# Cross-attention on one core: the output projection on split operands with source parts of their own, linear sums two blocks side by side, context loads issued by ScalarE, one place per tile

## The chip, the core and the metric

The kernel runs on one core of one Trainium2 chip. Its time is the device time of one execution in microseconds, and the number compared is the median of several executions. An engine has its own instruction queue and meets the others only at semaphores. The names here: PE or TensorE (matmuls), DVE (VectorE), ACT (ScalarE), POOL (GpSimd), SP (SyncE, which here only issues DMAs).

## The reference

Four batches of 1024 rows of width 512, and a context of the same size. First a 16-head softmax attention of x over the context, with an output projection, a residual and a layer norm; then a linear attention of the result over the same context, with a residual and a second layer norm.

```python
# first layer
Q, K, V = x @ Wq.T + bq, ctx @ Wk.T + bk, ctx @ Wv.T + bv      # 16 heads of 32
att = softmax(Q K^T / sqrt(32));  out = (att V) @ Wo.T + bo
x = layernorm(out + x) * gamma0 + beta0
# second layer
Q_phi, K_phi = elu(x), elu(ctx)
KV = einsum('bnd,bne->bde', K_phi, ctx)
Z = 1 / (Q_phi . K_phi.sum(axis=1) + 1e-6)
x = layernorm(x + (Q_phi @ KV) * Z) * gamma1 + beta1
```

All is float32. Where products must be both quick and accurate, the kernel splits an operand into a high part, rounded to the form fp32r, and a low part (the rest), and adds three products: high x high, high x low, low x high.

## The kernel before, in words

A **unit** is one batch, one group of four heads (128 columns) and one chunk of 256 rows of x: 4 x 4 x 4 = 64 units. A unit has 16 **ticks**, numbered k over the whole run (1024, named HALVES). In a tick TensorE does one product of scores for the row maxima (`pass1`, L464, 512 columns), and 26 ticks later (LEAD) one pair of transposed scores (`pass2`, L478, 2 x 256 columns); ACT takes the exponential of the latter into a ring `p_ring` (L640), DVE the maximum of the former (L775). Three score banks and two transposed-score banks lie between the engines. Every eight ticks TensorE makes a `visit`: the weighted values of four exponentials (L496) and their row sums (L503), for which POOL adds pairs of `p_ring` (L1036) and pairs of pairs (L1043; DVE does half, L813).

Everything else is put **beside** the score products, at most one piece in a tick, none in a visit's tick. A planner in plain Python, run when the kernel is built, writes this order. It knows chains with a number of pieces (LENGTH): K, V, Q projections (4, 4 and 2), O the output projection of a tile of 128 rows (4), T the transposes of its features (1), A its linear attention (4), S a block of 128 rows of the linear sums KV (8), N the total of the context features (1), B the bias through Wo (4). A chain writes one of two PSUM banks, `misc`, in turn. Of the chains that are ready it takes the one with the earliest deadline; `earliest` and `deadline` are given in ticks. `book` puts the steps of DVE, ACT and POOL into ticks where a budget has room, `send` does so for SP's DMAs; `bulk` transfers are kept out of ticks 2 to 7 of each unit and out of ticks 13 to 23. Every engine's program is a loop over k that emits what is booked there, so a wait in one instruction holds up all that follows it on its engine.

**Keys and queries** go through DRAM to be stacked as high, low and high rows: `put_keys` (L1202) after ACT's `k_high` and DVE's `k_low`, then `stack_keys` (L1210); `put_queries` (L1171) and `stack_queries` (L1179). The row maxima take the same road (L1187, L1192).

**Linear sums**: `context_features` on ACT makes relu and exp of a 128 x 128 block of `ctx_nat` into `f_sb` (L713, L716), on DVE the elu into `fphi_sb` (L952); `sum_kv` on TensorE is one fp32 product for each of 8 context tiles (L574), for 4 blocks of each batch; POOL adds the features into `phi_total` (L1090, L1094). `load_context` on SP (L1220) brings a batch's eight tiles once; ACT waits for all eight before the first feature.

**Output projection**: `normalise` on DVE transposes and inverts the row sums through `den_rows` and writes `outT`, a ring of 19 units (L835). `o_project` (L549) multiplies it in full fp32 by `wo`, `sum_y` (L874) adds x and the bias, which POOL has added to x (L1050). The first norm, the features `e_sb` (ACT, L682 and L687; DVE, L911), the `dot` with `phi_total` (L917, which writes its unused products over x_nat), T (L557), A (L566, three fp32r products each piece) and the second norm follow. A tile holds two places, `x_nat` and `y_sb`, in three slots, and in the last batch four more slots in `ctxT_sb`; the last four of the eight last tiles reuse slots:

```python
slot_of = [tile % NX for tile in range(TILES - KT)] + [NX, NX + 1, NX + 2, NX + 3, 0, 1, 2, NX]
```

## Time and profile before

| what | value |
|---|---|
| median of 3 runs | 1534.6 us (1530.89 to 1534.61) |
| profiled execution, its own time | 1535.64 us |
| its span | 1534.0 us |
| mean granted clock of TensorE | 0.996 |
| TensorE busy | 1495.3 us (97%) |
| VectorE, ScalarE, GpSimd busy | 1200.1, 825.5, 1130.6 us |
| data moved by DMA | 170.16 MB |

The span is the time from the first to the last instruction. A busy share says how long an engine had an instruction in it, also while that instruction was held up; which engine sets the pace of a stretch is seen in the stretch, and in the chain of work that ended last, which is followed back from the last instruction.

### The profile page before, as it was taken

What the parts mean: (1) busy time and instruction counts of PE and PEld (TensorE: products, weight loads), DVE (VectorE), ACT (ScalarE), POOL (GpSimd) and SP (SyncE); (2) the same over time, 40 slices, a digit from 0 to 9 for tenths busy, and PEclk for the clock granted to TensorE, in tenths of its full rate; (3) what the DMA queues carried; (4) which work ended last, traced back from release to release, by engine and by line L of the source; (5) the groups of instructions that cost most, each with busy time, mean ns of one, the idle gap of its engine ahead of it and who ended that gap; (6) DMA issues with size and microseconds to landing.
All of it is one profiled execution on the core that took longest, in us unless ns stands there. A gap on an engine that the chain in (4) does not pass through costs nothing.

```text
span 1534.0 us, 30583 instructions
## 1 busy us (share of the span) xinstructions
PE 1495.3 (97%) x11040; PEld 1053.0 (69%) x11040; DVE 1200.1 (78%) x2445; ACT 825.5 (54%) x1595; POOL 1130.6 (74%) x1036
## 2 busy tenths in 40 slices
PE   8899999999999999999999999999999999999986
PEld 6666767676766767667677777766767677756653
DVE  6577787767787887977787787888677778798987
ACT  2454565545555555665555555656555555565542
POOL 0366676757888787957678888876678887796995
PEclk9999999999999999999999999999999999999999
DMA  6735164352434245253343534325342342421001
GB/s 219 200 122 148 55 184 127 120 134 86 129 93 131 84 127 155 59 145 118 102 107 98 143 93 131 122 90 142 102 139 76 119 133 87 143 65 34 14 23 41
DMA packets 159573, 170.16 MB, mean 111 GB/s; under 512 B 20288, under 2 KB 122048, under 8 KB 159424
## 3 DMA queue, kind: packets, MB, share of 16 engines
q1 hardware_dynamic: 157696, 167.16, 36.8%
q8 instruction: 88, 1.44, 0.4%
q10 hardware_dynamic: 1728, 1.05, 0.2%
q14 instruction: 61, 0.50, 0.1%
HBM read 125.97 MB, written 42.21 MB: 110 GB/s over the span
## 4 chain that ended last, share of the span: by engine, by line
PE 85%; DVE 4%; POOL 4%; DMA 3%; issue 2%; ACT 1%; SPq 1%; DVEq 0%; POOLq 0%; ACTq 0%
PE score L464 15%; PE scoreT L478 14%; PE acc L496 14%; PE misc L537 7%; PE misc L513 7%; PE misc L526 6%; PE misc L574 6%; PE misc L549 6%; PE misc L566 5%; PE acc L503 3%; POOL pair_sum L1036 2%; DVE maxes L775 1%; PE misc L557 1%; DMA k_dram<-k_low 1%; DMA ctx_nat<-ctx_in 1%
## 5 line engine op out<-in xcount | busy, mean ns | idle before, releaser
L640 ACT ACTIVATE p_ring<-scoreT 128x512 f32<-128x512 f32 x1024 | 596.9, 595 | 572.1 <-PE scoreT L478 568.5
L1036 POOL TENSOR_TENSOR pair_sum<-p_ring 128x512 f32<-128x512 f32 x512 | 659.7, 1301 | 306.8 <-DVE pair_sum L813 165.0
L775 DVE TENSOR_REDUCE maxes<-score 128x1 f32<-128x512 f32 x1024 | 683.7, 680 | 196.5 <-PE score L464 190.7
L464 PE MATMUL score<-k_stack,q_stack 96*128 96x512 f32 x1024 | 601.0, 588 | 4.8 <-DVE maxes L775 1.8
L478 PEld LDWEIGHTS scoreT<-q_stack,k_stack 104*128 104x128 f32 x2048 | 387.2, 191 | 160.9 <-ACT p_ring L640 87.7
L478 PE MATMUL scoreT<-q_stack,k_stack 104*128 104x256 f32 x2048 | 419.2, 286 | 9.3 <-ACT p_ring L640 8.6
L464 PEld LDWEIGHTS score<-k_stack,q_stack 96*128 96x128 f32 x1024 | 193.1, 189 | 158.0 <-issue 109.8
L496 PE MATMUL acc<-p_ring,v_sb 128*32 128x256 f32 x4096 | 247.6, 382 | 0.0
L496 PEld LDWEIGHTS acc<-p_ring,v_sb 128*32 128x32 f32 x4096 | 120.0, 109 | 83.4 <-issue 0.4
L1043 POOL TENSOR_TENSOR pair_sum<-pair_sum 128x512 f32<-128x512 f32 x128 | 165.7, 1295 | 0.0
L537 PE MATMUL misc<-wv,ctxT_sb 128*128 128x128 f32 x1024 | 134.5, 274 | 0.0
L526 PE MATMUL misc<-ctxT_sb,wk 128*128 128x512 f32 x256 | 131.4, 596 | 1.9 <-DMA ctxT_sb<-ctxT_in 1.7
L574 PE MATMUL misc<-ctx_nat,fphi_sb 128*128 128x512 f32 x256 | 131.9, 596 | 0.2 <-DVE fphi_sb L952 0.2
L513 PE MATMUL misc<-xT_sb,wq 128*128 128x256 f32 x512 | 131.5, 379 | 0.2 <-DVE k_low L863 0.2
L549 PE MATMUL misc<-wo,outT 128*128 128x512 f32 x256 | 129.8, 592 | 1.0 <-DVE ctxT_sb L932 1.0
L537 PEld LDWEIGHTS misc<-wv,ctxT_sb 128*128 128x128 f32 x1024 | 125.9, 191 | 0.8 <-issue 0.5
L813 DVE TENSOR_TENSOR pair_sum<-pair_sum 128x512 f32<-128x512 f32 x128 | 113.1, 883 | 2.6 <-POOL pair_sum L1036 2.5
L513 PEld LDWEIGHTS misc<-xT_sb,wq 128*128 128x128 f32 x512 | 88.6, 189 | 8.4 <-issue 0.5
L952 DVE SCALAR_TENSOR_TENSOR fphi_sb<-f_sb,ctx_nat 128x128 f32<-128x128 f32 x128 | 85.9, 671 | 3.0 <-ACT f_sb L716 1.9
L503 PE MATMUL acc<-pair_sum,ones 128*32 128x256 f32 x1024 | 78.9, 380 | 3.7 <-DVE pair_sum L813 3.1
L1068 POOL TENSOR_TENSOR tiles<-tiles,gamma_row 128x512 f32<-128x512 f32 x52 | 70.0, 1345 | 9.3 <-ACT tiles L673 9.3
L1094 POOL TENSOR_TENSOR phi_total<-phi_total,fphi_sb 128x128 f32<-128x128 f32 x96 | 51.0, 531 | 25.8 <-DVE fphi_sb L952 25.0
(95 smaller groups left out, 1361.8 us busy)
## 6 DMA issues: line engine op xcount, KB each, us to landing
xT_sb<-xT_in SPq DMA_DIRECT2D x63, 512.0 KB, 3.9
q_stack<-q_dram SPq DMA_DIRECT2D x189, 128.0 KB, 2.5
k_stack<-k_dram SPq DMA_DIRECT2D x93, 256.0 KB, 4.5
ctx_nat<-ctx_in SPq DMA_DIRECT2D x32, 256.0 KB, 4.1
q_dram<-q_high SPq DMA_DIRECT2D x63, 128.0 KB, 1.7
q_dram<-q_low SPq DMA_DIRECT2D x63, 128.0 KB, 1.9
k_dram<-k_high SPq DMA_DIRECT2D x31, 256.0 KB, 2.0
k_dram<-k_low SPq DMA_DIRECT2D x31, 256.0 KB, 2.1
```

What stands on the lines that cost most here:

```text
L464: pe.matmul(score[k % 3][:], q_stack[0:SPLIT, unit % NQ, j, t * P:(t + 1) * P], k_stack[0:SPLIT, group_of[unit] % 2 * QUAD + j, h * HALF:( ...
L478: mm = pe.matmul(scoreT[k % 2][:, (j % 2) * CH:(j % 2 + 1) * CH], k_stack[0:ROWS, group_of[unit] % 2 * QUAD + j, kt * P:(kt + 1) * P], q_s ...
L496: mm = pe.matmul(acc[j * DK:(j + 1) * DK, 0:CH], v_sb[:, group % 2, kt, j * DK:(j + 1) * DK], p_ring[:, n % NP, j * CH:(j + 1) * CH], star ...
L513: mm = pe.matmul(bank_of("Q", unit)[:, 0:CH], wq[:, t, :], xT_sb[:, unit % 2, t, :], start=t == 0, stop=t == G - 1)
L526: mm = pe.matmul(bank_of("K", i)[:], wk[:, t, :], ctxT_sb[:, h, t, :], start=t == 0, stop=t == G - 1)
L537: mm = pe.matmul(bank_of("V", i)[:, t * P:(t + 1) * P], ctxT_sb[:, h, f, t * P:(t + 1) * P], wv[:, f, :], start=f == 0, stop=f == G - 1)
L549: mm = pe.matmul(bank_of("O", tile)[:], outT[:, unit % NO, t % TPC * P:(t % TPC + 1) * P], wo[:, g, :], start=g == 0, stop=g == G - 1)
L574: pe.matmul(bank_of("S", i)[:], fphi_sb[:, piece % NPHI, :], ctx_nat[:, t, :], start=t == 0, stop=t == KT - 1).then_inc(T["kv_piece"], 1)
L640: act.activation(p_ring[:, n % NP, h * HALF:(h + 1) * HALF], scoreT[k % 2][:], ACT.Exp, scale=SCALE).then_inc(A["exped"], 1)
L775: dve.reduce_max(maxes[:, unit % 2, t, j, h:h + 1], score[k % 3][:], AX.X).then_inc(V["maxed"], 1)
L1036: pool.tensor_tensor(pair_sum[:, place_of_pair(pair), cols], p_ring[:, (n - 1) % NP, cols], p_ring[:, n % NP, cols], ALU.add).then_inc(L[" ...
L1043: pool.tensor_tensor(first, first, second, ALU.add).then_inc(L["quad_low"], 1)
```

## The change

1. **Output projection on split operands.** `wo` becomes `wo_high` and `wo_low`, made once after B from four raw blocks (ACT copies, DVE subtracts). For each tile ACT copies its four 128-column blocks of `outT` to `o_high` and DVE subtracts to `o_low`, booked six and five ticks ahead of the tile's first product. `o_project` issues three fp32r products for each block. `outT` is now a ring of five groups, so that a tile's four blocks may wrap and then take two instructions; the row sums' transposes write into it directly. The parts have buffers of their own (in the last batch `k_high` and `k_low` serve as a second pair), and a tile's products may start only after the one before it has ended and the copy is made.
2. **Linear sums two blocks side by side.** S is 2 chains a batch of 16 pieces, two products for each context tile, one in each `misc` bank; no other chain holds a bank meanwhile. Features are 128 x 256, made in place in `fphi_sb`. There is a pause of three ticks after half of a chain, and a chain starts only if no Q, K or V is due within 20 ticks.
3. **Loads issued by ScalarE.** `ctx_nat` is a ring of four tiles instead of a batch's eight. SP loads the first four, ACT the other 60, each awaited alone. Each context tile is thus loaded twice.
4. **One place per tile.** x, y and the result share one place; NX is 4, and the last eight tiles have a place each. The dot writes over `e_sb`, and so it waits for T, and the planner books it after T instead of ahead of it.
5. **Order.** Bulk transfers are kept out of ticks 13 to 29 instead of 13 to 23; O may start 33 instead of 28 ticks after the first transposed scores of its unit; the four raw blocks of Wo are four DMAs. The total N uses four 32-row products side by side in place of one of 128 rows. Small tensors are merged into one.

The core of the diff:

```diff
     UB = G * NC
     TILES = B * KT
     HALVES = 2 * KT * UNITS
-    NQ, NP, NO, NX = 3, 7, 19, 3
+    NQ, NP, NO, NX, NCTX = 3, 7, 5, 4, 4
     NPHI = 3
+    EXTRA, LAST_SLOTS = 8, [NX, NX + 1, NX + 2, NX + 3, NX + 4, NX + 5, NX + 6, NX + 7]
+    S_FIRST, S_GAP = 52, 96
+    SPLIT_LEAD, S_PAUSE = 6, 3
     VISIT = 4
     VISITS = KT * UNITS // VISIT
 
@@ -46,6 +49,12 @@
     def half_of(i):
 
         return i // (QUAD * TPC), i // TPC % QUAD, i % TPC
...
+        wo_high = sb("wo_high", [P, G, D], F32R)
+        wo_low = sb("wo_low", [P, G, D], F32R)
...
-        outT = sb("outT", [P, NO, CH])
+        outT = sb("outT", [P, NO, NC, CH])
         kv_high = sb("kv_high", [P, G, D], F32R)
         kv_low = sb("kv_low", [P, G, D], F32R)
-        f_sb = sb("f_sb", [P, 2, P])
-        fphi_sb = sb("fphi_sb", [P, NPHI, P])
+        fphi_sb = sb("fphi_sb", [P, NPHI, CH])
         phi_total = sb("phi_total", [P, D])
-        ctx_nat = sb("ctx_nat", [P, KT, D])
-
-        tiles = sb("tiles", [P, 2, NX, D])
-        x_nat = [*(tiles[:, 0, i, :] for i in range(NX)), *(ctxT_sb[:, 0, i, :] for i in range(4))]
-        y_sb = [*(tiles[:, 1, i, :] for i in range(NX)), *(ctxT_sb[:, 1, i, :] for i in range(4))]
+        o_high = [sb("o_high", [P, G, P], F32R), k_high[:].rearrange("p (g c) -> p g c", g=G)]
+        o_low = [sb("o_low", [P, G, P], F32R), k_low[:].rearrange("p (g c) -> p g c", g=G)]
+        ctx_nat = sb("ctx_nat", [P, NCTX, D])
+
+        tiles = sb("tiles", [P, NX, D])
+        tile_sb = [*(tiles[:, i, :] for i in range(NX)), *(ctxT_sb[:, i // G, i % G, :] for i in range(KT))]
         e_sb = sb("e_sb", [P, 2, D])
 
+        wo_raw = [*(tiles[:, g, :] for g in range(NX)), e_sb[:, 0, :]]
...
-        LENGTH = {"K": 4, "V": 4, "Q": 2, "O": 4, "T": 1, "A": 4, "S": 8, "N": 1, "B": 4}
+        LENGTH = {"K": 4, "V": 4, "Q": 2, "O": 4, "T": 1, "A": 4, "S": 16, "N": 1, "B": 4}
...
-            while k in steps or room["SP"].get(k, 0) + transfers > 3 or bulk and (k >= UT and 2 <= k % UT < 8 or 13 <= k < UT + 8):
+            while k in steps or room["SP"].get(k, 0) + transfers > 3 or bulk and (k >= UT and 2 <= k % UT < 8 or 13 <= k < UT + 14):
...
+        for step in range(NCTX):
+            send("ctx", 36, step)
...
-            return max(UT * unit_at[G * b + G - 1, t // TPC] + LEAD + 28, spaced if b < B - 1 else 0)
+            return max(UT * unit_at[G * b + G - 1, t // TPC] + LEAD + 27 + SPLIT_LEAD, spaced if b < B - 1 else 0)
...
+                for name, engine, ahead in (("o_high", "ACT", SPLIT_LEAD), ("o_low", "DVE", SPLIT_LEAD - 1)):
+                    when.setdefault(name, {})[start_of["O", i] - ahead] = i
+                    take(engine, start_of["O", i] - ahead, 7)
...
+                if ("N", i // KT) in end_of:
+                    dot_of[i] = book("dot", "DVE", max(end, end_of["N", i // KT] + 1) + 1, 13, i)
+                else:
+                    undotted.append(i)
...
+                if kind == "S" and any(other in "QKV" and deadline(other, j) < k + 20 for other, j in waiting):
+                    return False
+                if k < earliest(kind, i) or banks and any(k < end_of[use] + 2 for use in uses[-2:][:2 if kind == "S" else 1] if len(uses) > 1):
...
+                if kind == "O" and i > 0 and k < end_of.get(("O", i - 1 - (i > TILES - KT)), k) + SPLIT_LEAD + 1:
+                    return False
...
+                if chain[0] == "S" and piece == 2 * NCTX:
+                    k += S_PAUSE
...
             def o_project(tile, g):
                 b, t = divmod(tile, KT)
-                unit = unit_at[G * b + g, t // TPC]
                 if g == 0:
-                    pe.wait_ge(V["out_scaled"], unit_at[G * b + G - 1, t // TPC] + 1)
+                    pe.wait_ge(V["o_low_kept"], tile + 1)
                     if tile == 0:
-                        pe.wait_ge(M["wo"], 16)
-                mm = pe.matmul(bank_of("O", tile)[:], outT[:, unit % NO, t % TPC * P:(t % TPC + 1) * P], wo[:, g, :],
-                               start=g == 0, stop=g == G - 1)
+                        pe.wait_ge(V["wo_low_kept"], G)
+                for term, (part, wo) in enumerate(((o_high, wo_high), (o_high, wo_low), (o_low, wo_high))):
+                    mm = pe.matmul(bank_of("O", tile)[:], part[place_of_tile(tile)][:, g, :], wo[:, g, :], start=g == 0 and term == 0,
+                                   stop=g == G - 1 and term == 2)
...
+            def sum_kv(i, piece):
+                t, d = divmod(piece, 2)
+                step = KT * i + t
+                if d == 0:
+                    pe.wait_ge(V["f_phi"], step + 1)
+                pe.matmul(bank_of("kv", 2 * i + d)[:], fphi_sb[:, step % NPHI, d * P:(d + 1) * P],
+                          ctx_nat[:, step % NCTX, :], start=t == 0, stop=t == KT - 1).then_inc(T["kv_piece"], 1)
...
+            def keep_o_high(tile):
+                b, t = divmod(tile, KT)
+                last = unit_at[G * b + G - 1, t // TPC]
+                act.wait_ge(V["out_scaled"], last + 1)
+                if tile == TILES - KT + 1:
+                    act.wait_ge(M["k_out1"], landed_keys(GROUPS - 1, 1, 2))
+                elif tile >= 1:
+                    act.wait_ge(T["o_projected"], tile - (tile > TILES - KT))
+                for gs, places in runs_of_places(b):
+                    copy = act.activation(o_high[place_of_tile(tile)][:, gs, :],
+                                          outT[:, places, t // TPC, t % TPC * P:(t % TPC + 1) * P], ACT.Copy)
+                copy.then_inc(A["o_high_kept"], 1)
+
+            def keep_wo_high(g):
+                act.wait_ge(T["bias_passed"], 1)
+                act.activation(wo_high[:, g, :], wo_raw[g], ACT.Copy).then_inc(A["wo_high_kept"], 1)
...
-            def context_features(piece):
-                d, t = piece // KT % G, piece % KT
-                if piece % (G * KT) == 0:
-                    act.wait_ge(M["ctx"], 16 * KT * (piece // (G * KT) + 1))
-                if piece >= 2:
-                    act.wait_ge(V["f_phi"], piece - 1)
-                act.activation(f_sb[:, piece % 2, :], ctx_nat[:, t, d * P:(d + 1) * P], ACT.Relu,
-                               scale=-1.0).then_inc(A["f_below"], 1)
-                act.wait_ge(A["f_below"], piece + 1)
-                act.activation(f_sb[:, piece % 2, :], f_sb[:, piece % 2, :], ACT.Exp,
-                               scale=-1.0).then_inc(A["f_grown"], 1)
+            def context_features(step):
+                cols = slice(step // KT % 2 * CH, (step // KT % 2 + 1) * CH)
+                act.wait_ge(M[f"ctx{step % NCTX}"], landed(step, NCTX, 1))
+                if step >= NPHI:
+                    act.wait_ge(T["kv_piece"], 2 * (step - NPHI + 1))
+                    i, before = divmod(step - NPHI, KT)
+                    act.wait_ge(L["totalled"], (KT - 1) * i + max(before, 1))
+                f = fphi_sb[:, step % NPHI, :]
+                act.activation(f, ctx_nat[:, step % NCTX, cols], ACT.Relu, scale=-1.0).then_inc(A["f_below"], 1)
+                act.wait_ge(A["f_below"], step + 1)
+                act.activation(f, f, ACT.Exp, scale=-1.0).then_inc(A["f_grown"], 1)
+
+            def load_context(step):
+                b, t = step // (2 * KT), step % KT
+                act.wait_ge(T["kv_piece"], 2 * (step - NCTX + 1))
+                act.dma_start(ctx_nat[:, step % NCTX, :], ctx[b, t * P:(t + 1) * P, :]
+                              ).then_inc(M[f"ctx{step % NCTX}"], 16)
...
+            def keep_o_low(tile):
+                b, t = divmod(tile, KT)
+                dve.wait_ge(A["o_high_kept"], tile + 1)
+                for gs, places in runs_of_places(b):
+                    part = outT[:, places, t // TPC, t % TPC * P:(t % TPC + 1) * P]
+                    low = dve.tensor_tensor(o_low[place_of_tile(tile)][:, gs, :], part,
+                                            o_high[place_of_tile(tile)][:, gs, :].bitcast(F32),
+                                            ALU.subtract)
+                low.then_inc(V["o_low_kept"], 1)
...
                 dve.wait_ge(A["ksum_kept"], tile // KT + 1)
+                dve.wait_ge(T["phi_turned"], tile + 1)
                 dve.tensor_tensor_reduce(
-                    out=x_nat[slot_of[tile]], in0=e_sb[:, tile % 2, :], in1=phi_total[:], scale=1.0, scalar=0.0,
+                    out=e_sb[:, tile % 2, :], in0=e_sb[:, tile % 2, :], in1=phi_total[:], scale=1.0, scalar=0.0,
                     op0=ALU.mult, op1=ALU.add, accum_out=z_sb[:, tile % 2, 0:1]).then_inc(V["dotted"], 1)
...
-            def load_context(first):
-                b, first = divmod(first, KT)
-                if b > 0 and first == 0:
-                    sp.wait_ge(T["kv_piece"], G * KT * b)
-                for t in range(first, first + 2):
-                    sp.dma_start(ctx_nat[:, t, :], ctx[b, t * P:(t + 1) * P, :]).then_inc(M["ctx"], 16)
+            def load_context(step):
+                sp.dma_start(ctx_nat[:, step, :], ctx[0, step * P:(step + 1) * P, :]).then_inc(M[f"ctx{step}"], 16)
...
+                    for g in range(G):
+                        sp.dma_start(wo_raw[g], WoT[g * P:(g + 1) * P, :]).then_inc(M["wo"], 16)
```

## Rows read from the trace of the kernel before

**Rows 1.** The page: busy time of each engine, and the chain that ended last by engine.
```profile
PE 1495.3 (97%) x11040; PEld 1053.0 (69%) x11040; DVE 1200.1 (78%) x2445; ACT 825.5 (54%) x1595; POOL 1130.6 (74%) x1036
...
PE 85%; DVE 4%; POOL 4%; DMA 3%; issue 2%; ACT 1%; SPq 1%; DVEq 0%; POOLq 0%; ACTq 0%
```

**Rows 2.** Stretches: width, then busy us (instructions) by engine, granted clock, DMA share, GB/s.
```profile
1180.00:1239.00 59.00, 58.99 (x433) 41.49 (x432) 46.54 (x98) 31.05 (x54) 45.13 (x42) 1.00 0.41 119
...
1416.00:1475.00 59.00, 55.93 (x427) 35.67 (x426) 54.37 (x102) 34.73 (x66) 54.84 (x50) 1.00 0.07 19
1475.00:1534.00 59.00, 40.89 (x222) 26.12 (x218) 42.26 (x87) 19.43 (x31) 42.24 (x41) 0.96 0.08 32
```

**Rows 3.** Timeline of TensorE before 90 us: start, us, line, operation, [idle before, releaser].
```profile
52.59 0.50 PE L478 MATMUL scoreT<-q_stack,k_stack 104*128 104x256 f32 x2 [3.01 <-ACT p_ring L640]
...
76.22 0.50 PE L464 MATMUL score<-k_stack,q_stack 96*128 96x512 f32 x1 [1.41 <-DMA q_stack<-q_dram]
...
80.57 0.79 PE L478 MATMUL scoreT<-q_stack,k_stack 104*128 104x256 f32 x2 [2.18 <-ACT p_ring L640]
```

**Rows 4.** Groups of instructions with shapes: count, busy us, mean ns, idle us before.
```profile
L775 DVE TENSOR_REDUCE maxes<-score 128x1 f32<-128x512 f32 x1024 | 683.7, 680 | 196.5 <-PE score L464 190.7
...
L549 PE MATMUL misc<-wo,outT 128*128 128x512 f32 x256 | 129.8, 592 | 1.0 <-DVE ctxT_sb L932 1.0
...
L813 DVE TENSOR_TENSOR pair_sum<-pair_sum 128x512 f32<-128x512 f32 x128 | 113.1, 883 | 2.6 <-POOL pair_sum L1036 2.5
...
L952 DVE SCALAR_TENSOR_TENSOR fphi_sb<-f_sb,ctx_nat 128x128 f32<-128x128 f32 x128 | 85.9, 671 | 3.0 <-ACT f_sb L716 1.9 <-issue 0.4 <-PE misc L574 0.4
...
L713 ACT ACTIVATE f_sb<-ctx_nat 128x128 f32<-128x128 f32 x128 | 39.1, 305 | 12.8 <-DVE fphi_sb L952 10.8 <-DMA ctx_nat<-ctx_in 1.8
...
L693 ACT ACTIVATE phiT_high<-misc 128x512 fp32r<-128x512 f32 x32 | 19.1, 596 | 7.4 <-PE misc L557 7.3
```

**Rows 5.** Chain that ended last, from 1437 us: start us, us, what.
```profile
1437.32 0.86 PE misc L549 x2
...
1438.65 0.86 PE misc L549 x2
...
1445.45 0.70 PE misc L566 x3
...
1446.62 0.69 PE misc L566 x3
```

**Rows 6.** L549 alone after 1455 us, columns as in rows 2.
```profile
1455.00:1534.00 79.00, 19.34 (x40) 6.79 (x40) 0.97 0.09 31
```

**Rows 7.** Timeline of SP's queue: context loads.
```profile
69.78 2.25 SPq L1220 DMA_DIRECT2D ctx_nat<-ctx_in  x4
```

**Rows 8.** Timeline of ACT: the first context features, the last exponential.
```profile
79.38 0.31 ACT L713 ACTIVATE f_sb<-ctx_nat 128x128 f32<-128x128 f32 x1 [1.78 <-DMA ctx_nat<-ctx_in]
...
1488.88 0.58 ACT L640 ACTIVATE p_ring<-scoreT 128x512 f32<-128x512 f32 x1
```

**Rows 9.** The stretch from 80 to 86 us, columns as in rows 2.
```profile
80.00:86.00 6.00, 5.43 (x16) 3.87 (x16) 4.81 (x14) 4.08 (x11) 3.60 (x4) 0.55 0.04 12
```

**Rows 10.** Chain that ended last, from 45 us.
```profile
45.25 6.09 DMA k_dram<-k_low
```

**Rows 11.** The page's DMA issues: count, KB each, median us from issue to landing.
```profile
k_dram<-k_low SPq DMA_DIRECT2D x31, 256.0 KB, 2.1
```

**Rows 12.** Timeline of the tail: DVE, then POOL, then TensorE.
```profile
1484.38 1.74 DVE L813 TENSOR_TENSOR pair_sum<-pair_sum 128x512 f32<-128x512 f32 x1 [2.19 <-POOL pair_sum L1036]
...
1499.63 0.42 DVE L835 TENSOR_TENSOR outT<-acc,den_rows 128x256 f32<-128x256 f32 x1
...
1478.90 1.74 POOL L1050 TENSOR_TENSOR ctxT_sb<-ctxT_sb,bo_row 128x512 f32<-128x512 f32 x1
...
1502.76 7.03 PE L549 MATMUL misc<-wo,outT 128*128 128x512 f32 x16
```

**Rows 13.** The tile ctx_nat: its loads from issue to landing.
```profile
DMA to landing us min/median/max: 2.6/4.1/7.8
```

245 lines of the change are left out of this document (134 added, 111 removed).

## The prediction

> **What bounds the kernel now.** I read the totals of the page and its chain first: TensorE is busy for 97% of the span and holds 85% of the chain that ended last; DVE and POOL hold 4% each [rows 1]. A busy share alone doesn't make a bound, so the table of stretches comes next: in the middle of the run TensorE is busy for 58.99 of 59 us while POOL has 45.13, DVE 46.54 and ACT 31.05; from 1416 us on POOL has 54.84 and DVE 54.37, and in the last stretch TensorE falls to 40.89 [rows 2]. So there are three regimes. From about 120 to 1450 us TensorE sets the pace and only its own work counts. After 1455 us, when the score products are over, the pace is that of POOL, DVE and the dependencies of the last tiles. And there are stalls before 90 us, which the timeline of TensorE shows one by one: 3.01, 1.41 and 2.18 us [rows 3].
>
> **The output projection.** Before: 32 tiles x 4 products of full fp32, 256 recorded instructions [rows 4]. After: 32 x 4 x 3 products of fp32r operands (high x high, high x low, low x high), the form in which L566 already runs. The chain gives both prices in the same surroundings, one step ("tick") of the order with one pass of scores and one of transposed scores around it: a tick with one L549 product lasts 1438.65 - 1437.32 = 1.33 us, a tick with three L566 products 1446.62 - 1445.45 = 1.17 us [rows 5]. The weight loads that each of the three brings are in the second figure. That is 0.16 us less for each product. After 1455 us stand 40 of the instructions, 20 products, so 108 before it [rows 6] and 108 x 0.16 = 17.3 us on the path. I take it whole.
>
> The Trainium skill (FP8 and Floating Point Precision, TensorE Precision Notes) counts true FP32 as four passes, which would make three passes three quarters of the price. The 0.86 us of L549 would become 0.645 and the gain 0.215 x 108 = 23.2 us; three L566 products measured 0.70, so the row decides, not the page.
>
> **The work that comes with it.** ScalarE copies a tile's four blocks to o_high, DVE subtracts to o_low: 32 of each, and 4 of each for wo. The nearest rows are 0.6 us for a 512-column ACT copy and, for DVE with two SBUF inputs, L813's mean of 0.883 [rows 4]. DVE: 36 x 0.883 = 31.8 us more. 24 tiles take two instructions each because the five places wrap; I put that at nothing beyond the crowding below. They stand six and five ticks ahead of the product, some 7 us for 1.5 to 2.4 us of work (0.6, and 0.883 to twice that), so in the middle they are covered. Without that cover each tile would cost TensorE up to 2.4 us, 77 us in all.
>
> **The linear sums.** Products stay the same: 128 in fp32. Features are made 256 columns wide: 64 steps instead of 128. Between L952's 0.671 (128 columns) and L813's 0.883 (512) I put 0.74 on DVE: 64 x 0.74 = 47 against 85.9, 38 less. POOL has 56 wider adds for 112 narrow ones, which is not more. ACT: relu and exp of 128 columns take 0.305 each, 512 columns 0.6, so 128 instructions of 256 columns at 0.40 for 256 at 0.305, 27 less; then 36 copies, 22 more, and 60 DMA issues, which no row shows on ACT in mid-run; SP's four contexts take 2.25 us to issue [rows 7], 0.56 each, 34 more, with 0 below and twice that above. Net: DVE about -7 us, ACT +29 of 1534, with 46% of ACT idle [rows 1, 4]. None is TensorE's, so none counts in the middle. The clue to what can go wrong is placement: a block of sums now holds both misc banks for 16 ticks plus a pause of three, with about two ticks empty before and one after. The number of empty ticks in the order doesn't change, they only come in clusters. An empty tick costs TensorE 1.33 - 0.86 = 0.47 us [rows 5] while DVE needs 0.68 for its maximum [rows 4]: 6 x 0.21 = 1.3 us in each of eight blocks, 10 at most, 0 if the three score banks absorb it. I take 2, nearer the absorbed end, because waits of TensorE for DVE are rare in this trace. A query projection can start up to some six ticks late behind a block; the round trip through DRAM is then still covered by the eight ticks that are left.
>
> **Context loads.** Before, all eight 256 KB tiles of a batch are awaited together; SP issues the last four from 69.78 to 72.03 us, and the first ACT instruction that needs them starts at 79.38, 1.78 us late [rows 7, 8]. TensorE stands 2.18 us behind that, and, idle twice within the six us before, it has a mean granted clock of 0.55 from 80 to 86 us, near the lower of its two levels (1.2 of 2.4 GHz): 6 x 0.45 = 2.7 us lost [rows 3, 9]. After, the first step needs the first tile alone, which is issued before those four, some 10 us ahead. I count 2.2 + 2.7 = 4.9 us back. The bulk transfers of ticks 24 to 29 move to tick 30, behind put_keys: in the chain the first key write took 6.09 us to land, behind the query stack, xT and wq, and the 3.01 us stall hangs on it; that of the 31 such writes is 2.1 in the median [rows 3, 10, 11]. With half as many context bytes ahead of it the query stack should land sooner too (1.41 us). But xT of the next unit is now issued some 5 us later and becomes what is late next. Bounds for the start: 0 and 2.2 + 2.7 + 3.0 + 1.4 = 9.3 us; I take 6, the context part and a quarter of the rest. The wo load is four issues instead of one, 3 x 0.56 = 1.7 us of SP [rows 7] ahead of the loads of the bias and gamma rows, which nothing awaits at that time: nothing.
>
> **The tail.** The last eight products, one stretch of 7.03 us, become 24 at 0.23 = 5.6 us: 1.4 back. The last bias add on POOL, 1.74 us in its crowded stretch, leaves the tail because every last tile has a place of its own: 1.7 back [rows 12]. Against it: each of the last tiles waits for copy and subtraction, 1.3 to 2.4 us (for the final pair the 2.7 us between the scaled output at 1500.05 and the product at 1502.76 cover it [rows 12]), its place in the order is five ticks later, about 1.0 us each where ticks have no score product, and the dot now follows the transpose on DVE. Bounds: -3 and +8 net; I take +2, since POOL and DVE, not the order, hold most of these ticks.
>
> **Sum:** -17.3 - 6 + 2 + 2 = -19.3 us. The profiled execution took 1535.64 (span 1534.0 and 1.6 around it), 1.0 over the median of 1534.6. 1535.64 - 19.3 = 1516.3, and on the scale of the median **1515.3 us**.
>
> **Rivals.** (a) All of the start and the tail come back too: -17.3 - 9.3 - 3 = -29.6, 1505 us. For it: each stall has one named transfer behind it. Against: a stall removed usually uncovers another at the start. Chance 0.16.
>
> (b) No measurable change. DVE has only 4.6 us to spare in 1416 to 1475, POOL 4.2 [rows 2]; about three tiles' subtractions fall there, each up to 1.74, and each also holds POOL up. With clusters at 10, the tail at +6 and the start giving nothing: -17.3 + 16 = -1, 1533 us. For it: an L813 of 0.883 in the mean took 1.74 beside a busy POOL at 1484 us [rows 12]. Against: the features give DVE 38 us back, a quarter of it at 1357 to 1430. Chance 0.09. The Trainium skill (SBUF — State Buffer, Who interferes with whom) says that a DVE instruction with two SBUF inputs contends with a GpSimd instruction that reads SBUF, and that is what o_low brings; the trace agrees with L813.
>
> (c) Slower. The ring of context tiles has four places. Tile s+4 is issued by ACT two ticks after step s starts its second half, and its features are due on ACT four ticks later. Where those ticks are the pause, that is only 1.33 + 3 x 0.47 = 2.8 us, and ACT may stand about 2.0 more (three ticks of 1.33, less some 2.0 of exponentials and features) before TensorE lacks an exponential: 4.8 us. The landing is 4.1 in the median and 7.8 at most [rows 13]. Two loads in each of eight blocks are that tight. If each took 7.8: 16 x 3.0 = 48 us, -19.3 + 48 = +29, 1563 us. It decides from 19.3 / 16 = 1.2 us each, a landing of 6.0. Against: outside the start the DMA queues are less than half busy, and the loads don't stand behind SP's. Chance 0.09.
>
> The forecast itself has 0.66; its own range is 1509 to 1524.
>
> **Numbers.** What this kernel's measurement can't tell from no change is 0.3%, 4.6 us. Faster: 0.66 + 0.16 = 0.82; same 0.09; slower 0.09. The range goes to (a) and into (b): 1504 to 1532.
>
> **What the profile after would show.** L549's successor: 384 instructions of fp32r, three of them 0.70 us in the chain, ticks of 1.17. TensorE still about 97% busy. No wait of ACT for ctx_nat after the start; if there is one of over 1 us several times, (c) is under way. No half clock between 78 and 86 us. The last exponential some 20 us earlier than the present 1488.88 [rows 8], and from it to the end a few us more or less than the present 45; a longer one means the later places of the tail's products. What would make the prediction wrong: waits of TensorE's score for DVE in the blocks of sums, late context tiles, or a tail more than 8 us longer.

## The result and the profile after

The changed kernel takes 1538.6 us (median; 1534.0 to 1543.8) where the kernel before takes 1534.6 (1530.9 to 1540.8) on the same chip: a ratio of 1.0024, 95% interval 1.0013 to 1.0034. That is inside the 0.3% that counts as no change, and on the slow side of it. 1515.3 was forecast.

The first rows to compare are those of the page: busy time by engine and the chain [rows 1].

```profile
PE 1485.9 (97%) x11192; PEld 1078.4 (70%) x11192; DVE 1216.3 (79%) x2443; ACT 828.1 (54%) x1526; POOL 1123.4 (73%) x977
...
PE 82%; DVE 8%; POOL 4%; ACT 2%; issue 2%; DMA 2%; SPq 0%; ACTq 0%; POOLq 0%; DVEq 0%
```

TensorE is busy 9 us less, and DVE's part of the chain has doubled from 4% to 8%. So a part of the gain was made, and waits for DVE are the first place to look for where it went. Next the forecast's own signs: groups with shapes, the chain, the timeline of TensorE before 90 us, and the stretches in the columns of rows 2.

```profile
L589 PE MATMUL misc<-wo_high,o_high 128*128 128x512 f32 x112 | 45.6, 407 | 0.5 <-DVE k_low L953 0.5
...
L1040 DVE SCALAR_TENSOR_TENSOR fphi_sb<-fphi_sb,ctx_nat 128x256 f32<-128x256 f32 x64 | 51.2, 800 | 0.3 <-ACT fphi_sb L782 0.3
```

```profile
1411.51 0.70 PE misc L589 x3
...
1412.68 0.69 PE misc L589 x3
...
1413.86 0.70 PE misc L589 x3
```

```profile
53.21 0.50 PE L504 MATMUL score<-k_stack,q_stack 96*128 96x512 f32 x1 [1.47 <-DMA q_stack<-q_dram]
...
75.89 0.51 PE L518 MATMUL scoreT<-q_stack,k_stack 104*128 104x256 f32 x2 [0.69 <-ACT p_ring L688]
...
77.63 1.10 PE L616 MATMUL misc<-ctx_nat,fphi_sb 128*128 128x512 f32 x2 [0.74 <-DVE fphi_sb L1040]
```

```profile
80.00:86.00 6.00, 6.00 (x58) 3.63 (x57) 5.89 (x8) 3.04 (x7) 4.87 (x5) 1.00 0.17 55
1180.00:1239.00 59.00, 58.01 (x426) 42.47 (x425) 54.13 (x107) 33.92 (x62) 51.90 (x47) 1.00 0.45 135
1416.00:1475.00 59.00, 51.71 (x427) 35.42 (x415) 51.45 (x94) 34.87 (x66) 53.72 (x46) 1.00 0.05 14
1475.00:1534.00 59.00, 40.19 (x216) 29.13 (x216) 47.05 (x100) 17.71 (x32) 35.56 (x36) 0.88 0.07 27
```

L589 has 384 instructions as forecast, 3 x 112 on `o_high` and `o_low` and 3 x 16 on the second pair; the line shown is the first of these groups. Three products stand in the chain with 0.70 us, ticks are 1.17 to 1.18 apart (1411.51, 1412.68, 1413.86) for 1.33 before [rows 5]. The start looks as forecast: where the 3.01 us stall was, TensorE now waits 1.47 us for the query stack; the 1.41 at 76 us is gone; the 2.18 has become 0.69 and 0.74; and the clock in 80 to 86 us is 1.00 for 0.55 [rows 3, 9]. The tail is not: in 1416 to 1475 us TensorE is busy for 51.71 us for 55.93 before [rows 2], and after the last exponential (1480.81 for 1488.88 [rows 8], 8 us earlier where some 20 were forecast) 55 us pass to the end of the span for 45.

And the middle, forecast at no loss, has this. TensorE, DVE and POOL around 530 us (start us, us, line, operation, [idle before, releaser]):

```profile
534.35 0.64 PE L543 MATMUL acc<-pair_sum,ones 128*32 128x256 f32 x8 [2.27 <-DVE pair_sum L890]
```

```profile
528.73 0.68 DVE L852 TENSOR_REDUCE maxes<-score 128x1 f32<-128x512 f32 x1
529.33 3.08 DVE L918 TENSOR_TENSOR o_low<-outT,o_high 128x512 fp32r<-128x512 f32 x1
532.33 0.68 DVE L973 BATCH_NORM_STATS2 norm_parts<-tiles 128x6 f32<-128x512 f32 x1
532.94 0.67 DVE L852 TENSOR_REDUCE maxes<-score 128x1 f32<-128x512 f32 x1
533.53 0.67 DVE L890 TENSOR_TENSOR pair_sum<-pair_sum 128x512 f32<-128x512 f32 x1
```

```profile
526.85 2.53 POOL L1126 TENSOR_TENSOR pair_sum<-p_ring 128x512 f32<-128x512 f32 x2
529.35 1.27 POOL L1133 TENSOR_TENSOR pair_sum<-pair_sum 128x512 f32<-128x512 f32 x1
530.58 1.27 POOL L1163 TENSOR_TENSOR tiles<-tiles,beta_row 128x512 f32<-128x512 f32 x1
```

Read it from the top: TensorE stands 2.27 us in a visit until DVE's half of a sum of four exponentials (L890, the pair of pairs) is there. That stands third behind the new subtraction, which took 3.08 us where its like takes 0.68 in a quiet place, while POOL ran one instruction after the other without a gap, to 531.85. The subtraction ends half a microsecond after that run.

**Where the time went, in numbers.** To see more than the worst places I took the start of every tick's first transposed product from the trace, and from each tick's length the median length of its kind (in the kernel before: 0.48 us with nothing beside the scores, 2.96 with a visit, 1.17 with three products of the attention, 1.33 with one product in fp32, and so on; a tick of the split projection at 1.17). What is left over is lost time. All is in us; the last column but one begins at transposed score 998 of 1024.

| kernel | until tick 60 | ticks 60 to 998 lost | then to the end | last tick of the order |
|---|---|---|---|---|
| before | 123.4 | 18.8 | 79.9 | 1095 |
| after | 122.8 | 37.3 | 90.2 | 1101 |

The work between tick 60 and 998 fell from 1311.9 to 1285.9 us: 17.3 by the products, and most of the rest because eight pieces of the sums stand before tick 60 now (at an equal time, so in this pair of traces the start gained some 6 us). Four products of a tile's linear attention have also moved behind tick 998; they take 2.8 us out of the middle and are a part of the tail's 10.3 without being lost. -0.6 - 26.0 + 18.5 + 10.3 = +2.2 us is the difference of the spans, 1536.2 and 1534.0. So the gain was eaten in two places: 18.5 us in the middle, 10.3 in the tail.

One trace is one execution, and that shows most at the start. The kernels of the next section that share the changed kernel's order and its work up to tick 60 reach that tick between 122.8 and 126.9 us; a kernel with the old start (the run before_one_later below) reaches it at 119.9, for 123.4 here.

### The profile page after: what moved, and what is told of

The parts are those of the page before. It is cut to its first block, busy times and chain, and to the rows that moved or that the text cites. A ratio compares the mean times of both kernels' runs of the same rounds, so it can differ in the third digit from the quotient of the medians.

```text
span 1536.2 us, 30636 instructions
## 1 busy us (share of the span) xinstructions
PE 1485.9 (97%) x11192; PEld 1078.4 (70%) x11192; DVE 1216.3 (79%) x2443; ACT 828.1 (54%) x1526; POOL 1123.4 (73%) x977
## 4 chain that ended last, share of the span: by engine, by line
PE 82%; DVE 8%; POOL 4%; ACT 2%; issue 2%; DMA 2%; SPq 0%; ACTq 0%; POOLq 0%; DVEq 0%
PE score L504 15%; PE scoreT L518 14%; PE acc L536 14%; PE misc L566 7%; PE misc L616 7%; PE misc L553 7%; PE misc L577 6%; PE misc L589 5%; PE misc L606 4%; PE acc L543 3%; DVE maxes L852 2%; POOL pair_sum L1126 1%; DVE o_low L918 1%; DVE pair_sum L890 1%; ACT k_high L709 1%
## 5 line engine op out<-in xcount | busy, mean ns | idle before, releaser
L504 PE MATMUL score<-k_stack,q_stack 96*128 96x512 f32 x1024 | 557.6, 546 | 7.3 <-DVE maxes L852 4.1
L890 DVE TENSOR_TENSOR pair_sum<-pair_sum 128x512 f32<-128x512 f32 x128 | 112.1, 876 | 2.8 <-POOL pair_sum L1126 2.7
L1158 POOL TENSOR_TENSOR tiles<-tiles,gamma_row 128x512 f32<-128x512 f32 x48 | 65.2, 1357 | 14.4 <-ACT tiles L721 14.4
L606 PE MATMUL misc<-kv_high,phiT_high 128*128 128x512 f32 x128 | 52.5, 410 | 6.8 <-issue 4.8
L1145 POOL TENSOR_TENSOR norm_parts<-norm_parts,small 128x1 f32<-128x1 f32 x64 | 45.7, 715 | 16.5 <-DVE norm_parts L980 16.5
L935 DVE SCALAR_TENSOR_TENSOR q_low<-misc,small,q_high 128x256 fp32r<-128x256 f32 x64 | 30.8, 481 | 33.8 <-ACT q_high L698 33.8
```

The source lines that it names most:

```text
L504: pe.matmul(score[k % 3][:], q_stack[0:SPLIT, unit % NQ, j, t * P:(t + 1) * P], k_stack[0:SPLIT, group_of[unit] % 2 * QUAD + j, h * HALF:( ...
L890: dve.tensor_tensor(first, first, second, ALU.add).then_inc(V["quad_high"], 1)
```

## The experiments

Theory 1 says that the subtractions and copies of the split crowd DVE. Theory 2 says that the paired linear sums and the new order cost the middle, whatever form the projection has. For the tail, Theory A blames the place in the order and Theory B the copies and subtractions themselves. All ratios are to the kernel before on the same chip, with 95% intervals; 0.1% is 1.5 us.

**full_o.** The projection goes back to one fp32 product from outT and wo; copies, subtractions and the lead go.

```
-    for term, (part, wo) in enumerate(((o_high, wo_high), (o_high, wo_low), (o_low, wo_high))):
-        mm = pe.matmul(bank_of("O", tile)[:], part[place_of_tile(tile)][:, g, :], wo[:, g, :], ...)
+    mm = pe.matmul(bank_of("O", tile)[:], outT[:, (G * b + g) % NO, t // TPC, ...], wo_sb[:, g, :], ...)
-    SPLIT_LEAD, S_PAUSE = 6, 3
+    SPLIT_LEAD, S_PAUSE = 1, 3
```

> The changed kernel with the output projection back in full fp32 (128 products; no o_high, o_low, wo_high, wo_low; the products need no lead). Everything else is changed: linear sums two blocks side by side, context by ScalarE, one place per tile, dot behind the transpose. Theory 1 (the subtractions and copies of the split crowd DVE and are what the middle and the tail lose): the rest of the change is neutral or a gain, so against the kernel before 1527 to 1534 us (the start's 7 back, the projection's 20.8 not). Theory 2 (the paired linear sums and the order cost the middle 17 us, whatever the projection's form): the changed kernel plus the products' 20.8 us, 1559 us; against the kernel before 1.016.

Measured: 1.0011 (1.0000 to 1.0022), 1538.1 us. Neither theory is met. It is 20 us below what theory 2 said, so the split as a whole, with its lead, gives nothing; yet it is above the band of theory 1, so the rest of the change, which was to give 6 us, gives nothing either.

**low_quarter, low_twice, low_last.** TensorE's instructions and order stay word for word. The first subtracts a quarter of the columns and leaves old values in the rest; the second subtracts twice, the second time after waiting for the first; the third puts the subtraction last in its tick.

```
-    part = outT[:, places, t // TPC, t % TPC * P:(t % TPC + 1) * P]
+    part = outT[:, places, t // TPC, t % TPC * P:t % TPC * P + w]      # w = 32 after tile 0
```

> The changed kernel with the subtraction o_low made on a quarter of its columns (32 of 128 of each block; for tile 0 all, so the rest holds old values, which changes the result). TensorE's work and every order stay the same. Theory 1: three quarters of the subtraction's time and of its meetings with POOL go, so more than half of the middle's 17 us come back and a part of the tail's 13: 1520 to 1530 us. Theory 2 (not the subtraction): within 3 us of the changed kernel, 1536 to 1539.

> The changed kernel with every subtraction o_low made twice. Theory 1: as much again as the subtraction costs now, plus 10 to 25 us: 1549 to 1564. Theory 2: the middle absorbs it; plus 0 to 6 us, mostly in the tail: 1539 to 1545.

> The changed kernel with the subtraction as the last instruction of its tick on DVE, behind the sums of four that TensorE's visits wait for, in place of ahead of them. Theory 1 in its narrow form (the subtraction delays the sum of four behind it in its own tick): 3 to 10 us faster than the changed kernel, 1529 to 1536. Theory 2, or the subtraction's whole load rather than its place: within 2 us of the changed kernel.

Measured: 0.9971 (0.9959 to 0.9983); 1.0217 (1.0198 to 1.0236); 1.0017 (1.0008 to 1.0027). Halving and doubling both answer, so theory 1 holds for its subject: against 1.0024 a quarter of the columns gives 8 us back, the second subtraction costs 30. Its place within the tick makes no difference that can be told from noise; the narrow form of the theory falls.

**full_o_lead6.** `SPLIT_LEAD = 6` in full_o: the fp32 projection in exactly the order of the changed kernel.

> The kernel of the run full_o (projection in full fp32), but its products keep the split's place in the order, so TensorE's order of ticks is piece for piece that of the changed kernel (last tick 1101; in full_o it is 1093, before 1095). Theory A (the tail's loss is the place in the order: tiles start later and six to eight more ticks stand behind the last score product): the tail lengthens by 8 to 12 us over full_o's, 1547 to 1551 us, and the split form then gains 9 to 13 us on it at an equal order. Theory B (the tail's loss is the copies and subtractions themselves on ScalarE and DVE, not the place): within 3 us of full_o, 1536 to 1541.

Measured: 1.0053 (1.0036 to 1.0070), 1543.6 us. The place in the order costs 0.42%, 6.4 us (give or take 3, by the two intervals), less than Theory A's 8 to 12 and more than B's none. Its trace is 6.8 us longer than full_o's. The tail is 8.0 longer (85.5 after tick 998 for 77.5), but the middle is 4.9 shorter, because eight of a tile's products have moved from it into the tail, so 3.1 remain. The other 3.8 stand before tick 60, where the two orders are the same; there TensorE's granted clock was at the lower level for 3.4 us twice in this trace and never in full_o's. At this equal order the split gains only 0.29%, 4.5 us, of its 20.5 (128 x 0.16).

**lead3, lead5, pause0, pause2.** Changes of the two constants, `SPLIT_LEAD, S_PAUSE` = 3, 3; 5, 3; 6, 0; 6, 2.

> The changed kernel with copy and subtraction three and two ticks ahead of the product in place of six and five. The order's last tick falls from 1101 to 1096 and one tile's products fewer stand behind the scores. Theory A: the tail gives back 5 to 9 us, the middle stays: 1529 to 1534 us. Theory B: within 2 us of the changed kernel, 1536 to 1540. If the short lead doesn't cover copy and subtraction, the projection's ticks wait in the middle, up to 1 us for each of 32 tiles: 1540 to 1565.

> The changed kernel with copy and subtraction five and four ticks ahead. Last tick 1097, so the tail gives back about 5 us as with the lead of three; there TensorE waited 21 us for the subtraction in 18 places. If these waits come from copy and subtraction needing four to five ticks where DVE is behind, most go at five: 1532 to 1537 us; if they need six, 1538 to 1545.

> The changed kernel without the pause of three ticks in a block of sums, so the context tile loaded at the ring's turn has about 3 x 0.5 to 1.3 us less before its features. By the planner this also brings the last tick from 1101 to 1095 at the split's lead of six. If late context tiles cost (the rival (c) of the prediction): ScalarE waits for them in every block, 5 us and more slower in the middle. If not, and Theory A holds: 1528 to 1534 us by the tail alone; by Theory B 1535 to 1540.

> The changed kernel with a pause of two ticks in place of three in a block of sums, split lead still six. By the planner the last tick falls from 1101 to 1095, as with no pause. The run without pause gave 6 us back in the tail and lost 4 in the middle, with ScalarE waiting 7.9 us for context tiles in six places. If two ticks cover those waits, only the tail's gain is left: 1531 to 1535 us. If the middle's loss there was one of order (which chain stands beside which), 1536 to 1541.

Measured: 1.0081 (1.0057 to 1.0104); 1.0013 (0.9998 to 1.0027); 1.0020 (1.0007 to 1.0033); 1.0015 (1.0004 to 1.0026). All four change TensorE's order too. They shorten the tail by 3 to 8 us, lose 1 to 8 us more before tick 998, and none comes out more than 0.11% ahead of the changed kernel. In lead3 the waits of TensorE (who <- for whom: us in total, times, longest) name a reason:

```profile
PE misc L589 <- DVE o_low L918: 15.1, 15, 2.3
```

Three ticks don't cover the split; six do. In pause0 the engine that waits is ACT:

```profile
ACT fphi_sb L780 <- DMA ctx_nat<-ctx_in: 7.9, 6, 3.0
```

Among ACT's waits in the changed kernel there is none for a context tile, with loads of 2.3/2.6/6.1 us (least, median, longest). So the late context tiles of rival (c) do occur without the pause. That they cost time is not shown: in pause2 ACT waits 0.5 us once for a context tile, and the middle loses 40.8 us for pause0's 41.7.

**no_split_work, copies_only.** Copies and subtractions are left out after tile 0, or the subtractions alone; the products then read tile 0's parts, so the result is another. TensorE's order and its products are those of the changed kernel.

```
 def keep_o_low(tile):
+    if tile > 0:
+        return
...
-    pe.wait_ge(V["o_low_kept"], tile + 1)
+    pe.wait_ge(V["o_low_kept"], 1)
+    pe.wait_ge(A["o_high_kept"], tile + 1)
```

> The changed kernel without the copies to o_high and the subtractions to o_low after tile 0 (every projection reads tile 0's parts, so the output is that of other numbers); TensorE's instructions and order are those of the changed kernel and its products wait for the scaled outputs alone. The kernel of full_o_lead6 has the same order with 128 fp32 products for 384 fp32r ones, 20.8 us more work. Theory 1 (the copies and subtractions are what takes the projection's gain away, about 16 us): 1543.6 - 20.8 = 1523 us, 1521 to 1526. Theory 3 (the faster projection runs into another bound, DVE's maxima and POOL's sums, whatever the copies do): 1530 us or more.

> The same with ScalarE's copies kept and only the subtractions left out after tile 0. Theory 1 with DVE as the culprit: within 3 us of the run without both, 1523 to 1527. If ScalarE's copies carry a part (they delay exponentials that TensorE waits for), it lies midway, 1528 to 1534.

Measured: 0.9927 (0.9912 to 0.9942) for both, 1524.8 and 1524.5 us. This settles the greater part. ACT's copies cost nothing that can be seen; the products give 1.26% at an equal order (0.9927 against 1.0053), 19.3 us; DVE's subtractions cost 0.97%, 14.9 us (each give or take some 3). In the traces 8 us of the 14.9 are in the middle, 5 of them in the visits (which lose 9.7 us for copies_only's 4.6), and 6 are in the tail. DVE's busy time differs by 35.8 us (1216.3 against this run's):

```profile
PE 1479.8 (97%) x11192; PEld 1074.4 (71%) x11192; DVE 1180.5 (78%) x2388; ACT 827.1 (54%) x1526; POOL 1119.6 (74%) x977
```

So a microsecond of DVE costs the kernel 0.42 on average; in low_twice the second 36.5 us cost 0.81 each; that price includes DVE's wait for the first subtraction before the second. And the place at 530 us, DVE and the next visit of TensorE without the subtraction:

```profile
530.91 1.89 DVE L891 TENSOR_TENSOR pair_sum<-pair_sum 128x512 f32<-128x512 f32 x1
```

```profile
532.95 0.64 PE L543 MATMUL acc<-pair_sum,ones 128*32 128x256 f32 x8 [0.49 <-DVE pair_sum L891]
```

Now it is the sum of four itself that meets POOL's run and takes 1.89 us; TensorE waits 0.49 for 2.27. The meeting was there already; the subtraction adds one in front.

**TensorE's clock after the waits.** A part of the price is paid after a wait is over. In the changed kernel another long subtraction stands at 899 us. The timeline of TensorE shows what follows, and so do the stretches (columns as in rows 2):

```profile
904.07 0.64 PE L543 MATMUL acc<-pair_sum,ones 128*32 128x256 f32 x8 [2.35 <-DVE pair_sum L890]
...
907.93 0.63 PE L589 MATMUL misc<-wo_high,o_high 128*128 128x512 f32 x1
...
909.56 0.40 PE L589 MATMUL misc<-wo_high,o_high 128*128 128x512 f32 x1
```

```profile
905.50:908.90 3.40, 3.40 (x12) 2.81 (x11) 1.78 (x3) 2.82 (x5) 3.30 (x5) 0.51 0.39 116
...
1485.80:1489.20 3.40, 3.40 (x8) 2.66 (x9) 3.12 (x5) 0.00 (x0) 3.40 (x4) 0.50 0.06 24
1499.50:1502.90 3.40, 3.40 (x10) 2.66 (x9) 3.29 (x8) 1.87 (x4) 0.67 (x2) 0.50 0.01 2
1516.50:1523.30 6.80, 4.44 (x12) 3.42 (x13) 5.62 (x16) 2.12 (x4) 1.28 (x2) 0.50 0.00 0
```

After a wait of 2.35 us TensorE works at the lower of its two clock levels (1.2 GHz for 2.4; the row has 0.51) for 3.4 us, and a product takes 0.63 us for 0.40. Not every such wait does it: none of this follows the 2.27 us at 534 in this trace. In the tail the clock is low three times before 1525 us, with 11.2 us of TensorE's work in these stretches (ahead of the first, from 1480 to 1485.8, TensorE was busy for 2.71 of 5.80 us); the kernel before and copies_only have one such stretch each there:

```profile
1498.50:1501.90 3.40, 3.40 (x9) 2.62 (x9) 1.46 (x5) 0.82 (x1) 3.30 (x5) 0.50 0.22 82
```

```profile
1499.10:1502.50 3.40, 3.31 (x8) 2.66 (x9) 1.30 (x2) 0.52 (x1) 1.92 (x3) 0.50 0.20 77
```

If half of the work's time at the lower level is lost and all of it is on the path, that is an estimate of 5.6 us against 1.7, so up to 4 of the 10.3 us by which the tail is longer than before, and up to 4 of the 6 by which it is longer than in copies_only. Over all executions the mean granted clock is 0.9958 in copies_only, 0.9932 in the changed kernel and 0.9865 in low_twice. The differences, times 1536 us, are 4.0 and 10.3 us: as an estimate that much, at most, of the prices of 14.9 and 29.6 us comes through the clock, and the rest is the waits themselves.

**low_one_input, low_on_pool, low_in_gap, low_in_gap_lead5.** What about the subtraction costs: its second input, its engine, its place?

```
-    low = dve.tensor_tensor(o_low[...][:, gs, :], part, o_high[...][:, gs, :].bitcast(F32), ALU.subtract)
+    low = dve.tensor_scalar(o_low[...][:, gs, :], part, 0.0001, None, ALU.mult)        # low_one_input
+    low = pool.tensor_tensor(...)                              # low_on_pool, tiles 0 to 23
...
+    lead = next((lead for lead in (6, 7, 8, 5, 9, 4, 10) if ... and
+                 (start_of["O", i] - lead + 1 - LEAD - 4) % 8 in (2, 3)), SPLIT_LEAD)   # low_in_gap
```

> The changed kernel with each subtraction replaced by a scaling of the same 512 columns on DVE (one SBUF input in place of two; o_low then holds other numbers). If the 14.1 us come from the meeting of a two-input DVE instruction with POOL's (3.0 us in place of 0.7 in the two worst places): the instruction stays near its shortest and most comes back, 1525 to 1529 us. If they come from any further instruction in DVE's order: 1533 to 1539.

> The changed kernel with the subtraction of the first 24 tiles made by POOL in place of DVE (place in the order six less one ticks ahead, as before; the last eight stay on DVE). TensorE's work is the same. The subtractions cost 14.1 us on DVE (1538.6 with them, 1524.5 without), some 8 of these before the last batch's stretch. If it is DVE's time that counts, and POOL's 27% of idle time takes them: 1528 to 1533 us. If POOL's sums of pairs fall behind instead, TensorE waits for them in the visits: 1537 to 1550.

> The changed kernel with copy and subtraction of 21 of the first 24 tiles moved by up to four ticks, so that the subtraction's tick is one of the two in eight (the third and fourth after a sum of pairs begins) in which POOL has no sum of pairs or of four booked. TensorE's order and all the work are the same. If the meeting with POOL's back-to-back sums is what makes the subtraction dear: the two places of 3 us (tiles 7 and 15) and most of the middle's 7.9 us go, 1530 to 1535 us. If any further DVE instruction costs as much wherever it stands: 1537 to 1540.

> The same with a split lead of five, which brings the order's last tick from 1101 to 1097 and one tile's products ahead of the last scores. lead5 alone measured 1537.2. If the two gains add up: 1527 to 1532 us, faster than both kernels. If the middle is saturated and only moves its losses: 1535 to 1539.

Measured: 0.9999 (0.9983 to 1.0014); 1.0057 (1.0041 to 1.0074); 1.0054 (1.0037 to 1.0071); 1.0018 (1.0003 to 1.0034). The one-input form gives 4 us back, a quarter of the cost; its trace gains nothing in the middle (37.2 us lost for 37.3) and 2.6 us in the tail. Here is the same step in three forms at the same three places: changed kernel, one input, a quarter wide (its first place is another quiet one).

```profile
332.80 0.68 DVE L918 TENSOR_TENSOR o_low<-outT,o_high 128x512 fp32r<-128x512 f32 x1
...
383.49 1.73 DVE L918 TENSOR_TENSOR o_low<-outT,o_high 128x512 fp32r<-128x512 f32 x1
```

```profile
383.41 1.47 DVE L918 TENSOR_SCALAR o_low<-outT 128x512 fp32r<-128x512 f32 x1
...
529.22 2.82 DVE L918 TENSOR_SCALAR o_low<-outT 128x512 fp32r<-128x512 f32 x1
```

```profile
351.62 0.28 DVE L919 TENSOR_TENSOR o_low<-outT,o_high 128x128 fp32r<-128x128 f32 x1
...
384.38 1.33 DVE L919 TENSOR_TENSOR o_low<-outT,o_high 128x128 fp32r<-128x128 f32 x1
...
530.19 2.69 DVE L919 TENSOR_TENSOR o_low<-outT,o_high 128x128 fp32r<-128x128 f32 x1
```

0.68, 1.73, 3.08 for the whole width and 0.28, 1.33, 2.69 for the quarter: the same 1.05 and 2.40 us of waiting on top, whatever the width (the one-input form takes 0.42 us in its quiet place at 332.92). That explains why a quarter of the columns still keeps 23.4 of 35.8 us of DVE's time. The Trainium skill (SBUF — State Buffer, Who interferes with whom) says that DVE and GpSimd share a pair of ports, that whoever issues first holds it for its whole instruction, and that a scaling of this kind can take the pair too. The trace agrees that the one-input form waits as well (1.47 and 2.82), and goes further: at 529 us DVE let not one but two following POOL instructions pass.

low_in_gap was to show whether this meeting is the whole of the cost, and it can't. The two worst places are cured (1.08 us for 3.08 at tile 7), but others became longer, and the subtractions take as long in all. Changed kernel, then low_in_gap:

```profile
L918 DVE TENSOR_TENSOR o_low<-outT,o_high 128x256 fp32r<-128x256 f32 (+3 forms) x48 | 44.9, 967 | 0.9 <-ACT o_high L746 0.8
```

```profile
L921 DVE TENSOR_TENSOR o_low<-outT,o_high 128x256 fp32r<-128x256 f32 (+3 forms) x48 | 45.0, 971 | 0.6 <-ACT o_high L749 0.6
```

The visits' loss fell from 9.7 us to 4.7, yet the middle lost 40.4 us in all for 37.3. A part of the waits is now at the score products (8.5 us for 4.1):

```profile
PE score L507 <- DVE maxes L855: 8.5, 15, 2.1
```

So the expectation of 1530 to 1535 failed. The meeting makes the instruction longer, and curing the worst places didn't lower the cost; how the 14.9 us divide between the meetings and the plain length of the instruction stays open. On POOL the subtraction helps nothing: the visits lose 11.4 us and the middle 40.5. I had no version left that beats the kernel before; the best of those that compute the same, lead5 and low_in_gap_lead5, are at 1.0013 and 1.0018.

**full_o_old_sums, full_o_dot_early, before_one_later.** What of the rest, in full fp32, costs the 6 us that the start was to gain? The first puts the unpaired sums, eight resident context tiles and SP's loads back, the second gives the dot a buffer of its own and its old place, the third is the kernel before with `LEAD + 221` for `LEAD + 220` in the tiles' earliest tick.

> The kernel of full_o (fp32 projection, nothing split) with the linear sums of the kernel before as well: one block at a time, 128 columns, all eight context tiles resident, loaded by SyncE. What is left of the change: places of tiles and outputs, dot behind the transpose, the start's window for bulk transfers. full_o's middle loses 7.1 us more than that of the kernel before and its start 6 us less. If the paired sums and what they move in the order are the cause of the middle's loss and of the start's gain: both go, 1533 to 1538 us, with the start's 2.2 us wait for features back. If the places and the dot are: the middle's loss stays and the start's gain goes, 1539 to 1545.

> The kernel of full_o with the dot written to a buffer of its own and booked ahead of the transpose, as in the kernel before. If the dot's late place costs (in the tail TensorE or DVE waits behind it): 1533 to 1536 us. If not, within 2 us of full_o's 1538.

> The kernel before with nothing changed but the earliest tick of the tiles of the first three batches, one tick later. It calibrates what chance in the order is worth. If a middle loss of 7 to 9 us as in full_o and full_o_old_sums can be chance of the order alone: this moves by 3 us or more either way, 1537 to 1543 most likely, since the old order was the better half. If it stays within 2 us of 1534: order chance is small, and the rest of the change has a cost of its own that stays open.

Measured: 1.0070 (1.0053 to 1.0086); 1.0040 (1.0024 to 1.0055) with a median of 1538.6, no more than 0.3% off full_o's and not faster; 1.0025 (1.0015 to 1.0035). Lost in the middle: 30.2, 24.4 and 24.0 us, for 25.9 in full_o and 18.8 before. The paired sums, with their loads by ACT, are not the loss: without them it is 1.0070 for 1.0011, with 4 us more lost in the middle and 2 in the tail. The later dot isn't the loss either, since its old place brings nothing (by the ratios it is even 0.29% slower, by medians on two chips equal). And one tick of delay in the tiles' earliest tick, after which the planner puts another piece into 87 of the first 1023 ticks, loses 5.2 us in the middle and 3.8 in all.

## Why the prediction was wrong, point by point

Against the sum -17.3 - 6 + 2 + 2, in us of the ratios:

| step | forecast | measured | by |
|---|---|---|---|
| the products, wherever they stand | -18.7 (17.3 + 1.4) | -19.3 | full_o_lead6 to copies_only |
| the copies on ACT | 0 | 0 | no_split_work, copies_only |
| the subtractions on DVE | 0 in the middle, a part of +2 in the tail | +14.9 | copies_only to after |
| the split's place in the order | within the same +2 | +6.4 | full_o to full_o_lead6 |
| all the rest | -6 and +2, less 1.7 in the tail | +1.7 | before to full_o |

1.7 + 6.4 - 19.3 + 14.9 = 3.7 us, 0.24%. The rows lead from one kernel to the next, so they add up by construction; each has an uncertainty of some 2 to 3.5 us from the intervals of its two ratios.

**The output projection** was right: the tick from 1.33 to 1.17, and the whole of it on the path. By the four passes of the Trainium skill (FP8 and Floating Point Precision, TensorE Precision Notes) the price would have been three quarters, and the gain larger than the measured one; the row decided rightly.

**The step that failed** is the sentence "They stand six and five ticks ahead of the product, some 7 us for 1.5 to 2.4 us of work ..., so in the middle they are covered." It asks whether the product waits for the subtraction, and it doesn't: at a lead of six no wait of L589 for `o_low` is among TensorE's. It doesn't ask who stands behind the subtraction on DVE. Behind it are the maxima that free the score banks and the half sums that every visit waits for. DVE's work was sized well, 31.8 us with wo, for 35.8 measured without; the price of 0 was wrong. Of the 14.9 us about 8 are in the middle (37.3 against 29.3 lost) and 6 in the tail (90.2 against 84.2). I let the 38 us that the features give back on DVE stand against it. They do come off DVE's sum (85.9 to 51.2), but in the ticks of the sums, not where the tiles are: from 1180 to 1239 us DVE is busy for 54.13 us, for 46.54 before [rows 2].

**The tail** was mis-sized. In the traces it is 10.3 us longer. I named most of its parts, bounded them at +8 and took +2, "since POOL and DVE, not the order, hold most of these ticks". full_o_lead6 has neither copies nor subtractions, and its place in the order alone costs 6.4 us over full_o, of which its trace has 3.1 outside the start. The term "five ticks later, about 1.0 us each" was the estimate to use; the planner then puts one tile more behind the last scores (last tick 1101 for 1093). The lower clock in the tail was no term of mine at all.

**The start** was right in place: the waits that it named are gone or shorter. Its size can't be told from these traces. At equal work the changed kernel is some 6 us ahead of the kernel before at tick 60, but only some 3 us ahead of before_one_later, which has the work and order of the kernel before there. Its trace has no 1.41 us stall, 1.03 us for the 2.18, and its one low clock of 3.4 us at 53.5 instead of 6.8 us at 78.6. So a part of the 4.9 us that I counted from one trace was a matter of that execution.

**The clusters of empty ticks** cost nothing to speak of: between tick 60 and 998 the blocks of sums, their pauses and edges included, lose some 3 us in all, 5 before. What took the start's gain is elsewhere in the middle, 7.1 us in full_o. 1.2 us of that is the total N, whose one product has become four of 32 columns (its tick is 1.67 us for 1.34, in each of four batches). For the rest I have a bound, not a cause: it isn't the paired sums nor the dot, and one tick's shift in the order before makes 5.2 us of the same kind. That it is chance of the order, or of the single trace, is argued, not shown; that full_o_old_sums is at 1.0070 leaves room for a cost of its own in the places and waits of tiles.

**The rivals.** (b) had the right outcome, and half of it the right ground: o_low beside a busy POOL, at 1.74 us in the tail. It gave the middle no more than the clusters, and had 0.09; at 1533 us it was still on the other side of the kernel before. (c) did not happen: with the pause no wait of ACT for a context tile is left. (a), at 1505 us, and the forecast of 1515.3 were both out of reach: even with the subtractions left out the kernel takes 1524.5.

## What to carry to other kernels

When an instruction is added to an engine that has slack on average, don't only ask whether its own result comes in time; list what stands behind it in that engine's order and who waits for that. Here DVE was 78% busy; each further microsecond cost the kernel 0.4, and the next 0.8. Look at the bounding engine's clock too: a wait can cost more than its own length. An order written by a planner moves in jumps: a longer lead moved a tile's products behind the last scores, and a shift of the tiles' earliest tick by one was worth 0.25%, so an expected gain of that size has to be measured against such shifts. Two kernels with the same order on the bounding engine, which differ in one piece of work, gave the clean prices; every run that also moved the order mixed two effects. And stalls and clock falls of one trace are those of one execution: before pricing them, look whether a second execution has them.
